# High and low parts of the activations interleaved in one tile of a multi-expert tower

## What is computed

```
xe = x[:, EXPERT_IN_IDX, :]                       # ten experts, two per task and two shared
eo = relu(einsum('bed,edh->beh', xe, W) + b)      # ten products 1024 x 1024
gates = softmax(einsum('btd,tdk->btk', x[:, :T], Gw) + Gb)
task_out = einsum('btk,btkh->bth', gates, eo[:, SEL, :])
shared_out = einsum('be,beh->bh', gs, eo)         # first layer only
h = relu(concat(z, dense_ctx) @ W_top1 + b_top1); h = relu(h @ W_top2 + b_top2); y = h @ W_top3
```

## Time and profile before

| | |
|---|---|
| median of three runs | 1985.26 us |
| profiled execution | 1986.03 us, span 1984.1 us |
| TensorE busy | 1975.7 us (100%) |
| VectorE busy | 1348.2 us (68%) |
| ScalarE busy | 703.5 us (35%) |
| mean DMA rate | 117 GB/s |
| granted TensorE clock | 0.999 of 2.4 GHz |

### The profile page before, as it was taken

One profiled execution on the slowest core, in us unless ns is written; L12 is line 12 of the kernel. 1 busy time (PEld: TensorE's weight loads), 2 busy tenths in 40 slices (PEclk: granted clock), 3 DMA queues, 4 the chain that ended last, 5 costly groups with the idle time before them and its releaser, 6 DMA issues.

```text
span 1984.1 us, 25306 instructions
## 1 busy us (share of the span) xinstructions
PE 1975.7 (100%) x8914; PEld 1613.2 (81%) x8914; DVE 1348.2 (68%) x1331; ACT 703.5 (35%) x934; POOL 168.9 (9%) x152
## 2 busy tenths in 40 slices
PE   8999999999999999999999999999999999999999
PEld 7878878888788888888878788788887888888887
DVE  4588988896256765667555888898942666566564
ACT  3233333334233333332434233323333332433333
POOL 4631000000030002122033000000000000000000
PEclk9999999999999999999999999999999999999999
DMA  6553324333253334343344334334332433333331
GB/s 214 169 165 114 127 87 137 120 106 101 85 152 108 117 94 150 106 141 119 100 145 138 125 95 135 96 122 130 101 102 74 123 95 125 98 117 95 117 95 43
DMA packets 69101, 232.24 MB, mean 117 GB/s; under 512 B 10036, under 2 KB 11324, under 8 KB 69032
## 3 DMA queue, kind: packets, MB, share of 16 engines
q1 hardware_dynamic: 60664, 210.30, 34.2%
q0 software_dynamic: 7488, 20.98, 3.3%
q10 hardware_dynamic: 880, 0.10, 0.0%
HBM read 230.27 MB, written 1.08 MB: 117 GB/s over the span
## 4 chain that ended last, share of the span: by engine, by line
PE 99%; DMA 0%; ACT 0%; issue 0%; POOL 0%
PE main L369 29%; PE main L371 29%; PE main L370 29%; PE top L370 3%; PE top L371 3%; PE top L369 3%; PE gps L422 1%; PE gps L434 1%; DMA eo_sh<-in_tbl,idx 0%; PE gps L409 0%; PE top L502 0%; PE top L560 0%; DMA idx<-in_ids 0%; ACT eo_b L793 0%; PE main L560 0%; PE gps L560 0%
## 5 line engine op out<-in xcount | busy, mean ns | idle before, releaser
L369 PE MATMUL main<-act_hi,w_hi 128*128 128x512 f32 (+1 forms) x2576 | 1002.2, 389 | 0.0
L371 PE MATMUL main<-act_hi,w_lo 128*128 128x512 f32 (+1 forms) x2576 | 1000.5, 388 | 0.0
L370 PE MATMUL main<-act_lo,w_hi 128*128 128x512 f32 (+1 forms) x2576 | 1000.5, 388 | 0.0
L930 DVE TENSOR_TENSOR w_lo<-raw,w_hi 128x1024 fp32r<-128x1024 f32 (+1 forms) x356 | 433.7, 1218 | 593.9 <-ACT w_hi L624 559.2
L624 ACT ACTIVATE w_hi<-raw 128x1024 fp32r<-128x1024 f32 (+1 forms) x356 | 376.5, 1058 | 1219.2 <-PE main L371 1103.8
L369 PEld LDWEIGHTS main<-act_hi,w_hi 128*128 128x128 f32 x2576 | 483.7, 188 | 107.7 <-issue 8.2
L371 PEld LDWEIGHTS main<-act_hi,w_lo 128*128 128x128 f32 x2576 | 483.5, 188 | 99.9
L370 PEld LDWEIGHTS main<-act_lo,w_hi 128*128 128x128 f32 x2576 | 483.7, 188 | 99.5
L1049 DVE TENSOR_TENSOR slots<-slots,prod 128x1024 f32<-128x1024 f32 (+2 forms) x202 | 245.0, 1213 | 6.0
L360 POOL DMA_INDIRECT slots<-in_tbl,idx x144 | 164.8, 1145 | 898.7 <-DVE act_lo L942 605.8
L1043 DVE TENSOR_TENSOR prod<-eo_sh,gate_b 128x1024 f32<-128x1024 f32 x136 | 165.7, 1219 | 1.7
(11 more groups left out here) (81 smaller groups left out, 418.5 us busy)
## 6 DMA issues: line engine op xcount, KB each, us to landing
raw<-in_w SPq DMA_DIRECT2D x304, 512.0 KB
gate_b<-tasks_dram SPq DMA_DIRECT2D x32, 512.0 KB
raw<-in_w_top SPq DMA_DIRECT2D x32, 512.0 KB
raw<-in_w_first SPq DMA_DIRECT2D x16, 512.0 KB
gate_b<-tasks_dram SPq DMA_DIRECT2D x16, 256.0 KB
slots<-in_tbl,idx POOLq DMA_INDIRECT x144
gate_b<-gates_dram SPq DMA_DIRECT2D x2, 512.0 KB
raw<-in_w_top SPq DMA_DIRECT2D x4, 256.0 KB
```

What stands on the lines that cost most here:

```text
L369: nc.tensor.matmul(dst, lhs_hi, rhs_hi, start=start, stop=False)
L370: nc.tensor.matmul(dst, lhs_hi, rhs_lo, start=False, stop=False)
L371: return nc.tensor.matmul(dst, lhs_lo, rhs_hi, start=False, stop=stop)
L930: nc.vector.tensor_tensor(w_lo[0:parts, slot, 0:cols], raw[0:parts, rawslot, 0:cols], w_hi[0:parts, slot, 0:cols], ALU.subtract).then_inc( ...
```

## The change

act_hi and act_lo were two tiles of their own. Now they are two views of one tile with a fourth axis of length two: element (k, n) of the high part lies next to element (k, n) of the low part. Nothing else differs; all instructions address the views as before, with a step of two elements along n.

```diff
-        act_hi = sb("act_hi", [P, KT, N], f32r)
-        act_lo = sb("act_lo", [P, KT, N], f32r)
+        act = sb("act", [P, KT, N, 2], f32r)
+        act_hi, act_lo = act[:, :, :, 0], act[:, :, :, 1]
```

## The result

The changed kernel takes 3897.52 us (median of six runs, 3897.22 to 3898.7) against 1985.0 us before, a ratio of 1.9635 (95% interval 1.9615 to 1.9655). The forecast was 3792 us; the time lies 105 us above it, inside the range.

The account below looks back on a forecast made before the run. TensorE was taken to bound the kernel: 1986.0 us profiled plus 1807.1 us for stepped products gave 3793.1, said as 3792 us (chance 0.60). The forecast's own range was 3680 to 3915 us, widened to 1983 to 3920 with no change.

Parts of the forecast that it names:

- The bound: Whole kernel: TensorE is 99% of the chain, so time is the number of matmuls times their spacing, 97% of the span.
- The price of a stepped column: All 8520 products: 0.833 ns a column plus 12.7 ns fixed, 439.4 ns for 226.7 at 512 columns; +1807.1 us in all.
- the upper end of the forecast's own range: Products: each plain product doubled whole, +226.7 ns at 512 columns and +119.7 at 256, up to 3915 us.
- The mechanism: Products' moving stream: two neighbouring words at every 1.2 GHz tick, so a step of two brings one useful word a fetch.
- No change: Products: two useful words still lie in every 16 bytes, so the step costs nothing and time stays 1985 us; chance 0.24.
- The rule of the Trainium skill: Products: at least two hits in a 16-byte line give full rate, so a step of two would leave 1985 us.
- The estimate after: Products: two words per 16-byte access of 1.73 ns, 0.865 ns a column, 0.456 us a product, some 3925 us.
- Late hand-overs: Hand-overs at 27 places: VectorE's strips take longer and weights' splits come late; 2001 us, or 2042; chance 0.04.
- The bound of 0.34 ns an element: Hand-over strips: upper price per stepped stream, from 183 against 172 ns copies; 0.35 us a strip on VectorE, 0.17 on ScalarE.
- ScalarE's stepped write, taken as nothing: Hand-overs, ScalarE writing act_hi strips: no cost expected, as one new word a tick is all the engine asks.
- Cover: Change at 193 us: 1.74 us free before TensorE needs the weights' split, growing as units go from 5.44 to 10.5 us.
- Plain f32 logits: L422 keeps 3.55 us for 32 records; stepped reads at L409 cost nothing, or 3.6 us more if doubled.

Follow-up runs that it names:

- e1_pairs: Changed kernel with the parts interleaved by two elements instead of one (two high words, two low words); 3898.25 us, ratio 1.9638.
- m4_lanes: Small program in place of the kernel: products reading two places by turns; fp32r 0.216 us, 0.232 with the layout's step of two, 0.453 with step four.
- e7: Changed kernel with products reading columns n and n + 256 by turns, ScalarE undoing the order out of PSUM, first unit unchanged; 1990.38 us, ratio 1.0026.
- m1_moving: Small program in place of the kernel: groups of 48 products with different moving access patterns; fp32r 0.232 us a product at step 1, 0.453 at step 2.
- e2_writers_stepped: Changed kernel with stepped writers kept, but products reading each strip's first and second 512 words without a step; 1985.32 us, ratio 1.0002.
- m2_writers: Small program in place of the kernel: VectorE subtractions and ScalarE copies with steps 1, 2, 4, 5; VectorE 686 ns at step 1, 684 at step 2.
- m3_moving: Small program in place of the kernel: more moving patterns in groups of 48 products; two fp32r places 8 KB apart by turns took 0.216 us a product.
- e6: Kernel before the change, two plain tiles, products reading columns n and n + 256 by turns, order undone out of PSUM; 1894.04 us, ratio 0.9541.

## Why the prediction was right, and where it was not

- **The bound** held: TensorE is the whole chain before and after, and the loss is the number of products times what each lost.
- **The price of a stepped column** was taken as 0.833 ns plus a fixed 0.0127 us a product, 439.4 ns. It measured 451.1. That is the mis-sized term: 11.7 ns x 8472 = 99 of the 105 us. It holds two errors that partly cancel. The stepped products of 512 and 256 columns differ by 451.1 - 226.7 = 224.4 ns, so a column costs 0.877 ns and not 0.833 (+22 ns a product), and 2 ns are left as a fixed part and not 12.7 (-10 ns). The fixed part read out of plain products of 512 and 256 columns did not carry over. 512 plain columns and 256 stepped ones take the same 0.2267 us, which fits that both make each lane go over 128 lines; the plain product doubled whole, the upper end of the forecast's own range, comes within 2.3 ns.
- **The mechanism** ("one useful word in each fetch of two neighbours") was wrong though its number was near, and that is luck: 0.833 ns was chosen because three rows of other work lay beside it, and the products lost half their rate for another reason. e1_pairs has neighbours and is as slow; m4_lanes and e7 have none and are fast. What the runs support in its place is a lane for the even and one for the odd columns, each bound by its 16-byte lines. Plain f32's pace of 0.87 ns a column, on which the choice leaned, does not depend on such fetches: m1_moving has 0.445 us a record without a step and 0.450 with step 2.
- **No change**: the rival said that two useful words in 16 bytes suffice. With a step of two they don't; by the lanes' account, because the two words belong to different lanes. With the order changed by e7 a lane has two words in each line, and then they do.
  The rule of the Trainium skill ("SBUF — State Buffer", Door 1: The DMA port swizzle) of two hits in a line is contradicted here for fp32r as it stands: two hits a line, and 0.4511 us instead of 0.2267. Counted lane by lane, two hits are enough.
  The estimate after "Vector Engine (DVE) Microarchitecture Reference" (Measured stream behaviour on trn2) of the Trainium skill, 0.456 us a product from its 1.73 ns for one source that hops at every element, came nearer than the forecast's 0.439. (The recorded 3925 us leaves out the 48 short products; with them it is 3930.) The same section of the Trainium skill asks for runs of adjacent words for the full rate, which doesn't hold for VectorE in m2_writers: step 2 has no such runs, and its subtraction takes 684 ns.
- **Late hand-overs** did not come: e2_writers_stepped is within 0.12% of the kernel before. The bound of 0.34 ns an element came from a copy with a step of five and says nothing of a step of two: m2_writers shows 0.74 ns an element for step 5 (1066 for 686 ns) and nothing for step 2. ScalarE's stepped write, taken as nothing, does cost 36 ns a strip, and nothing waits for it.
- **Cover** grew as said. At a change of the changed kernel, VectorE ends the split of the next weights at 372.55 us and TensorE needs it at 379.65:

```profile
371.32 1.23 DVE L930 TENSOR_TENSOR w_lo<-raw,w_hi 128x1024 fp32r<-128x1024 f32 x1 [0.89 <-ACT w_hi L624]
379.65 0.63 PE L369 MATMUL main<-act,w_hi 128*128 128x512 f32 x1
```

  That is 7.1 us where it was 1.74. VectorE now waits for ScalarE at L942, 112.8 us in all, because ScalarE in turn waits for slower products to free the strips.
- **Plain f32 logits** at L422 kept their 3.54 us, and those that read the parts with the step (L409) take 29.40 - 25.60 = 3.80 us to the next product where they took 3.61: close to nothing, as said.

## What to carry to other kernels

In fp32r, look at a moving operand by its even and its odd columns: each of the two sets should find as many of its words as it can in every 16-byte line, and a step of two in plain order halves the rate for every product. Reading a strip from its start and its middle by turns (n and n + N/2), and undoing the order where the sums leave PSUM, took 4.6% off a kernel bound by such products and made an interleaved layout nearly free. The same reading of two plain tiles stays the faster one by 96 us (1894 and 1990 us). A fixed part worked out of two sizes of one pattern must be checked on the pattern that it is used for.

## What the runs showed of the hardware that was not expected

- A contiguous fp32r stream is not at its fastest: 0.2267 us for 512 columns, where reading from start and middle needs 0.2158. By the lanes' account its lines bound it.
- bf16 went otherwise: steps of 1, 2, 4 and 8 elements took 0.217, 0.225, 0.451 and 0.900 us for 512 columns, as one lane with 1.76 ns a line would. In m3_moving the expectations for bf16 at steps 3, 5 and 6 held within 1% (0.340, 0.563, 0.676 us), and steps 16 and 32 took 0.918 and 0.857 where 0.90 was expected. Plain f32 took 0.445, 0.450 and 0.891 us a record at steps 1, 2 and 4. Yet in two places by turns they took 0.485 and 0.535; how these streams fetch is open.
- A stationary operand with a step of two cost nothing (0.232 us, as without).
- ScalarE read PSUM with a step of two columns at the same pace as without: 0.476 and 0.478 us from one copy to the next. Reading PSUM in order and writing the two halves of the SBUF tile by turns took 0.878 us, so in e6 and e7 it matters that the order is undone on the PSUM side.
